# Transposing u of chunks 3 to 7 by VectorE's blocks and sixteen DMAs, with the next x product ahead of the new chunk's gates

## What is computed

```
t   = rmsnorm(x, norm1_w)
xb  = causal_depthwise_conv(t @ Wx, conv_w, conv_b)          # 4 taps
h   = rg_lru(xb, Wi, Wa, lam)                                # gates by sigmoid, a scan along the tokens
h1  = x + (h * gelu(t @ Wy)) @ Wo
u   = rmsnorm(h1, norm2_w)
ffn = (gelu(u @ Wg) * (u @ Wu)) @ Wd                         # Wg, Wu: 256 x 1024
x1  = layernorm(x + h1 + ffn)
out = layernorm(x1 + relu(x1 @ W1 + b1) @ W2 + b2)           # W1: 256 x 1024
```

## Time and profile before

| what | value |
|---|---|
| median of three runs | 587.22 us (586.84 to 587.23) |
| the profiled execution | 587.02 us |
| its span, first to last instruction | 585.2 us |
| TensorE busy | 578.5 us (99%) |
| VectorE, ScalarE, GpSimd busy | 401.0, 314.6, 203.8 us |
| granted TensorE clock, mean | 0.998 |

### The profile page before, as it was taken

How to read it: one execution, slowest core, us unless ns; L and a number is a source line. 1 busy time by engine, 2 the same in 40 slices (tenths; PEclk the granted TensorE clock), 3 DMA queues, 4 the chain that set the end, 5 groups by cost and what they waited for, 6 DMA issues and landing times.

```text
span 585.2 us, 9307 instructions
## 1 busy us (share of the span) xinstructions
PE 578.5 (99%) x3441; PEld 511.9 (87%) x3441; DVE 401.0 (69%) x729; ACT 314.6 (54%) x600; POOL 203.8 (35%) x282
## 2 busy tenths in 40 slices
PE   8999999999999999999999999999999999999996
PEld 8768988898888988898888888889888898888996
DVE  5888958867739668495765848568595765563565
ACT  7977675834548444573446634575343843232454
POOL 2111336273233542255233452424523233140130
PEclk9999999999999999999999999999999999999999
DMA  7400210011100121001210031100200010101011
GB/s 275 149 36 25 84 36 2 2 29 44 37 0 1 27 84 36 1 1 38 73 37 0 1 82 38 26 2 8 65 22 16 1 34 5 34 3 37 1 38 36
DMA packets 27197, 21.46 MB, mean 37 GB/s; under 512 B 3448, under 2 KB 26384, under 8 KB 27152
## 3 DMA queue, kind: packets, MB, share of 16 engines
q1 hardware_dynamic: 27152, 20.87, 11.8%
HBM read 10.89 MB, written 4.19 MB: 26 GB/s over the span
## 4 chain that ended last, share of the span: by engine, by line
PE 97%; DVE 1%; POOL 0%; issue 0%; ACT 0%; DVEq 0%; POOLq 0%; ACTq 0%
PE psum L454 18%; PE psum L456 18%; PE psum L455 18%; PE psum L465 11%; PE psum L467 11%; PE psum L466 11%; PE psum L545 2%; PE psum L472 1%; PE psum L838 1%; PE psum L510 1%; PE psum L676 1%; PE psum L678 1%; PE psum L674 1%; PE psum L572 1%; PE psum L529 1%; PE psum L489 0%
## 5 line engine op out<-in xcount | busy, mean ns | idle before, releaser
L1903 POOL TENSOR_SCALAR gu_hi<-gu_raw 128x512 fp32r<-128x512 f32 x64 | 54.4, 851 | 262.0 <-DVE gu_raw L1514 262.0
L1092 ACT ACTIVATE hid_raw<-psum,vecs 128x512 f32<-128x512 f32 x56 | 38.4, 686 | 115.4 <-PE psum L456 115.3
L1514 DVE TENSOR_TENSOR gu_raw<-psum,gu_raw 128x512 f32<-128x512 f32 x64 | 44.0, 687 | 69.9 <-PE psum L456 69.9
L1524 DVE TENSOR_TENSOR hid_lo<-hid_raw,hid_hi 128x512 fp32r<-128x512 f32 x56 | 40.7, 728 | 47.2 <-ACT hid_hi L1096 47.2
L465 PE MATMUL psum<-w_d_hi,gu_hi 128*128 128x256 f32 x256 | 72.2, 282 | 0.0
L465 PE MATMUL psum<-w_hi,hid_hi 128*128 128x256 f32 x256 | 71.9, 281 | 0.2 <-DVE hid_lo L1524 0.2
L467 PE MATMUL psum<-w_d_hi,gu_lo 128*128 128x256 f32 x256 | 71.8, 281 | 0.0
L467 PE MATMUL psum<-w_hi,hid_lo 128*128 128x256 f32 x256 | 71.8, 281 | 0.0
L466 PE MATMUL psum<-w_lo,hid_hi 128*128 128x256 f32 x256 | 71.7, 280 | 0.0
L466 PE MATMUL psum<-w_d_lo,gu_hi 128*128 128x256 f32 x256 | 71.7, 280 | 0.0
L1077 ACT ACTIVATE gu_raw<-psum 128x512 f32<-128x512 f32 x64 | 38.1, 595 | 50.3 <-PE psum L456 49.7
(11 more groups left out here) (237 smaller groups left out, 1530.7 us busy)
## 6 DMA issues: line engine op xcount, KB each, us to landing
out_dram<-row SPq DMA_DIRECT2D x15, 256.0 KB, 2.4
xs<-in_L_attn_x_dram SPq DMA_DIRECT2D x7, 512.0 KB, 3.7
gy<-normed SPq DMA_DIRECT2D x96, 32.0 KB, 1.9
t_raw<-t_blocks SPq DMA_DIRECT2D x80, 32.0 KB, 1.9
raw_gud<-in_L_attn_Wg_dram SPq DMA_DIRECT2D x1, 1024.0 KB, 8.1
raw_gud<-in_L_attn_Wu_dram SPq DMA_DIRECT2D x1, 1024.0 KB, 10.2
raw_gud<-in_L_attn_Wd_dram SPq DMA_DIRECT2D x1, 1024.0 KB, 12.4
raw_gud<-in_L_ffn_W_dram SPq DMA_DIRECT2D x1, 1024.0 KB, 6.6
```

What stands on the lines that cost most here:

```text
L1092: nc.scalar.activation(raw, hidden, ACT.Relu, bias=vec("b1", m)).then_inc(relu_ready, 1)
L1514: nc.vector.tensor_tensor(gu_raw[:, r % SLOTS, :], up_bank(r)[:, :], gu_raw[:, r % SLOTS, :], ALU.mult).then_inc(gu_ready, 1)
L1524: nc.vector.tensor_tensor(hid_lo[:, w % SLOTS, :], hid_raw[:, w % SLOTS, :], hid_hi[:, w % SLOTS, :].bitcast(FP32), ALU.subtract).then_inc ...
L1903: nc.gpsimd.tensor_scalar(gu_hi[:, r % SLOTS, :], gu_raw[:, r % SLOTS, :], 1.0, 0.0, ALU.mult, ALU.add).then_inc(gu_hi_ready, 1)
```

## The change

For chunks 3 to 7, `transpose_u` and the splits from PSUM are gone. VectorE makes u's 32x32 blocks into a new buffer, sixteen DMAs on SyncE's queue put them in place in another, and ScalarE and VectorE split u from there. The new buffers lie over `mT_hi` and `mT_lo`. The tokens of u come out in the order of the blocks; gelu of the gate and gate times up put them back in order (`in_order`, `by_token`). Around it steps are moved:

- `mix_x(n + 1)` stands at the end of round 7 of the period before, ahead of the new chunk's first gate; for that t of chunk n + 1 is made in round 4 (`norm_t`, blocks, DMAs) and split in round 6.
- `mix_y(n)` stands in round 4 between `up` and `down`.
- `norm_u` stands ahead of `gate_hi` on GpSimd in round 6.
- the statistics of the second layer norm go from round 4 to round 6, its normalising from round 6 to round 7.
- the first gate of a chunk waits for one low half of u before its first k step, and for the other before its second.

```diff
+        with nc.sbuf_tensor("u_blocks", [P, KD, T], FP32) as u_blocks, nc.sbuf_tensor("u_raw", [P, KD, T], FP32) as u_raw:
+            pass
         mT_hi = sb("mT_hi", [P, KD, T], FP32R)
...
+        def move_blocks(queue, src, dst, moved):
...
+            for i in range(GROUPS):
+                for j in range(GROUPS):
...
+                    queue.dma_start(placed[rows_out, :, i, :], blocks[rows_in, :, j, :]).then_inc(moved, DMA)
...
+            def move_u(c):
+                sync.wait_ge(u_blocks_ready, KD * (c - BLOCKWISE + 1))
+                move_blocks(sync, flat(u_blocks), flat(u_raw), u_blocks_moved)
...
                 if c >= 4:
+                    move_u(c - 1)
                     store_out(c - 4)
             for c in range(CHUNKS - 4, LAST - 1):
                 move_x1(c + 1)
+                if c + 3 < CHUNKS:
+                    move_u(c + 3)
                 store_out(c)
...
                 if m == 0:
-                    pe.wait_ge(uT_lo_ready, 2 * c + 2)
+                    pe.wait_ge(uT_lo_ready, 2 * c + (1 if c >= BLOCKWISE else 2))
...
-                product(gate_bank(r)[:, :], "g", m, uT_hi, uT_lo).then_inc(gate_done, 1)
+                for k in range(KD):
+                    if m == 0 and k == KD - 1:
+                        pe.wait_ge(uT_lo_ready, 2 * c + 2)
+                    last = product_step(gate_bank(r)[:, :], "g", m, k, uT_hi, uT_lo)
+                last.then_inc(gate_done, 1)
...
                     up(r)
+                if mixing and m == 4 and p >= 2:
+                    mix_y(n)
                 if mixing and m == 3 and p >= 1:
                     mix_decay(n)
-                if mixing and m == 7 and p >= 2:
-                    transpose_u(n)
...
-                if mixing and m == 0 and p >= 2:
+                if r == 2 * KH:
                     mix_x(n)
-                if mixing and m == 4 and p >= 1:
+                if m == 7 and p >= 2 and n + 1 < CHUNKS:
+                    mix_x(n + 1)
+                if r == KH + 4:
                     mix_y(n)
...
+            def split_u_hi(c):
+
+                act.wait_ge(up_done, KH * c)
+                act.wait_ge(u_blocks_moved, MOVES * (c - BLOCKWISE + 1))
+                for f in range(KD):
+                    nc.scalar.activation(uT_hi[:, f, :], u_raw[:, f, :], ACT.Copy).then_inc(uT_hi_ready, 1)
...
+                    if m == 6 and p >= 2 and n + 1 < CHUNKS:
+                        split_t_hi(n + 1)
...
+                    if m == 7 and p >= 2:
+                        split_u_hi(n)
...
+            def transpose_u_blocks(c):
+                dve.wait_ge(u_ready, u_tiles(c))
...
+                if m == 6 and second:
+                    statistics(s, 1, 0, s2_ready)
+                    statistics(s, 1, 1, s2_ready)
                 if units(r):
                     gate_times_up(r)
+                if m == 6 and p >= 2 and n + 1 < CHUNKS:
+                    split_t_lo(n + 1)
+                if m == 6 and mixing and p >= 2:
+                    transpose_u_blocks(n)
...
                     hidden_lo(w)
+                    if m == 4 and p >= 2 and n + 1 < CHUNKS:
+                        transpose_blocks(n + 1)
+                    if m == 7 and mixing and p >= 2:
+                        split_u_lo(n)
...
-                if p == 1 and m == 7:
+                if mixing and m == (7 if p == 1 else 6):
                     norm_u(n)
                 if r < UNITS:
                     gate_hi(r)
...
+                if m == 4 and p >= 2 and n + 1 < CHUNKS:
+                    norm_t(n + 1)
```

More of the change, by code:

```diff
@@ L381, in store_out @@
                                    rows[c % 2][:, 2 * q:2 * q + 2, :]).then_inc(out_stored[c % 2], DMA)
[L383 to L393, removed]
             def move_t(c):
                 sync.wait_ge(t_blocks_ready, KD * (c - BLOCKWISE + 1))
-                move_blocks(flat(t_blocks), flat(t_raw), t_blocks_moved)
+                move_blocks(sync, flat(t_blocks), flat(t_raw), t_blocks_moved)
             def move_x1(c):
                 sync.wait_ge(x1_blocks_ready, KD * c)
-                move_blocks(flat(normed), flat(gy), x1_blocks_moved)
+                move_blocks(sync, flat(normed), flat(gy), x1_blocks_moved)
+            def move_u(c):
+                sync.wait_ge(u_blocks_ready, KD * (c - BLOCKWISE + 1))
+                move_blocks(sync, flat(u_blocks), flat(u_raw), u_blocks_moved)
             for q in range(PAIRS):
@@ L1076, in gelu_gate @@
                     act.wait_ge(gu_lo_ready, r - SLOTS + 1)
-                nc.scalar.activation(gu_raw[:, r % SLOTS, :], gate_bank(r)[:, :],
+                dst, gate = gu_raw[:, r % SLOTS, :], gate_bank(r)[:, :]
+                if r >= KH * BLOCKWISE:
+                    dst, gate = by_token(dst), in_order(gate)
+                nc.scalar.activation(dst, gate,
                                      ACT.Gelu_apprx_tanh).then_inc(gelu_ready, 1)
@@ L1175, in round_of @@
                 mixing = n < CHUNKS
-                if mixing and m == 1:
+                if r == 2 * KH + 1 or r == KH + 1:
                     conv_start(n, 1)
@@ L1184, in round_of @@
                 if mixing:
-                    if m == 0 and p >= 2:
+                    if m == 6 and p >= 2 and n + 1 < CHUNKS:
+                        split_t_hi(n + 1)
+                    if r == 2 * KH:
                         split_t_hi(n)
@@ L1307, in transpose_blocks, with split_u_lo @@
                                         ).then_inc(t_blocks_ready, 1)
+            def transpose_u_blocks(c):
+                dve.wait_ge(u_ready, u_tiles(c))
+                for k in range(KD):
+                    nc.vector.transpose(u_blocks[:, k, :].rearrange("p (j t s) -> p t j s", j=GROUPS, t=TT),
+                                        normed[:, :, k * P:(k + 1) * P].rearrange("p t (j s) -> p t j s", j=GROUPS)
+                                        ).then_inc(u_blocks_ready, 1)
+            def split_u_lo(c):
+                for f in range(KD):
+                    dve.wait_ge(uT_hi_ready, 2 * c + f + 1)
+                    nc.vector.tensor_tensor(uT_lo[:, f, :], u_raw[:, f, :], uT_hi[:, f, :].bitcast(FP32),
+                                            ALU.subtract).then_inc(uT_lo_ready, 1)
             def transpose_x1_blocks(c):
-                dve.wait_ge(uT_done, 2 * (c + 2))
+                if c + 1 < BLOCKWISE:
+                    dve.wait_ge(uT_done, 2 * (c + 2))
+                else:
+                    dve.wait_ge(u_blocks_ready, KD * (c + 2 - BLOCKWISE))
                 dve.wait_ge(x1_ready, TT * c + TT)
@@ L1672, in round_of @@
                     split_x1_lo(f)
-                if m == 6 and second:
+                if m == 7 and second:
                     normalise(s, 1, 0, out_ready)
@@ L1691, in round_of @@
                         statistics(f, 0, 1, s1_ready)
-                if m == 4 and second:
-                    statistics(s, 1, 0, s2_ready)
-                    statistics(s, 1, 1, s2_ready)
                 if r == FROM:
@@ L1863, in norm_u @@
                 rms(h1_squares(c), ss2, h1_squared, rms2_ms, rstd2, rms2_rstd)
-                pool.wait_ge(uT_done, 2 * c)
+                if c <= BLOCKWISE:
+                    pool.wait_ge(uT_done, 2 * c)
+                else:
+                    pool.wait_ge(u_blocks_ready, KD * (c - BLOCKWISE))
                 if by_blocks(c - 2):
```

29 lines of the change are left out of this document (15 added, 14 removed).

## The result

The changed kernel takes 630.72 us (median of four runs, 627.63 to 631.67) against 587.23 for the kernel before beside it: 1.073 times as long, 95% interval 1.069 to 1.077. The forecast was 626.3. The profiled execution took 631.58 us, its span 629.8, against 587.02 and 585.2: 44.6 us more. The mean granted clock fell from 0.998 to 0.971.

The account below looks back on a forecast made before the run. TensorE's own work was taken to bound the kernel (97% of the chain). Profiled 587.0 - 4.4 (transposes) + 12.0 (Wo wait) + 23.7 (u wait) + 8 (clock) = 626.3 us, range 612 to 638.

Parts of the forecast that it names:

- its likeliest case: Whole kernel: both waits come and TensorE's clock mostly falls at the gates, 626.3 us with its bounds; chance 0.58.
- Transposes: TensorE: forty transposes of u removed from the chain, 0.87 us a chunk in five chunks, 4.4 us saved.
- Product with Wo: Round 5: early Wy delays relu, root, scan and low part; TensorE waits 2.4 us in five periods, 12.0 us.
- u: First gate of a period: TensorE waits for u's low part, 4.2 us four times and 6.9 once, 23.7 us.
- the quick norm: GpSimd's norm of u taking 3.31 instead of 4.47 us: gate waits of 3.0 and 5.7, together 17.7 us.
- The clock: TensorE after gate waits: clock falls, 2.0 us lost after the long wait, 1.5 after each of four others, 8 us.
- The long wait: Gate wait of the last period (chunk 7), without a next x product: 6.9 us, charged 2.0 us of clock.
- The sentence on the Trainium skill: TensorE's clock falling 5.2 us after the last matmul: only the 6.9 us wait would cost, 2.0 not 8, sum 620.3.
- the clock holds: Rival: both waits come, but TensorE's clock stays up or returns at once, 618.3 to 620.3 us; chance 0.22.
- only u: Rival: no wait ahead of Wo, because the relu's release does not set the root, 614.3 us; chance 0.07.
- only Wo: Rival: SyncE issues faster, u's leg is covered, 594.6 us, 2.7 more if chunk 7 lacks cover; chance 0.05.
- faster: Rival: TensorE's two waits a period sum to less than the 0.87 us saved, its deciding point; 582.6 us; chance 0.04.

Follow-up runs that it names:

- e7: The changed kernel with round 4 reordered, seven of u's DMAs on ScalarE's queue, t's low part later, nine extra matmuls before the last gate: 589.45 us, 1.0039 times before.
- e8: As e7, but chunk 7's u transposed by TensorE, no extra matmuls, and round 5's gate times up behind Wo's low part: 584.60 us against 587.13, 0.9956 times before.
- e1: The kernel before with only the Wy product of chunks 3 to 7 moved between up and down of round 4: 603.13 us, 1.0275 times before.
- e4: The changed kernel with round 4 reordered: root ahead of relu on ScalarE, t's blocks and scan ahead of hidden split on VectorE: 620.02 us, 1.056 times before.
- e5: The changed kernel with the x product back at its old place behind the gate: 642.40 us, 1.0935 times before.
- e2: The changed kernel with six of u's sixteen DMAs issued from ScalarE's queue instead of SyncE's: 605.06 us, 1.029 times before.
- e3: The changed kernel plus 30 unread identity matmuls (45 in the last period) on TensorE ahead of each period's first gate: 632.80 us, 1.076 to 1.081 times before.
- e6: As e3, with 15 unread identity matmuls (22 in the last period) in place of 30 (45): 622.67 us, 1.060 times before.

## Why the prediction was right, and which term was too small

The forecast, 626.3 in 612 to 638, held the measured 630.72, and its likeliest case is the one that came. Step by step:

- **Transposes, -4.4.** The rows of eight end with chunk 2 in the trace after. That they were worth their 0.87 us is borne out by the sums of e7 and e8, which close with them to 0.0 and 0.6 us.
- **Product with Wo, 12.0.** Measured 12.4 (2.45 to 2.5 a period). Relu, root and low part are each where the prediction put them, e1 shows that Wy's place alone does it, and e4 that the link is the order behind the relu, on ScalarE and VectorE together. That t's blocks add nothing was right as well: they fill the hole in which VectorE waits for the root (e1).
- **u, 23.7.** Measured 22.7. The leg in p = 3 is 1.84 + 4.39 + 1.34 + 12.9 = 20.5 us against 20.77 forecast, TensorE's cover 16.6 as forecast. That the norm's leg came out so near (4.39 against 4.47) is partly luck: its small steps took 1.50 us where the row used had 2.18, its four tiles 2.80 where it had 2.29. The last period was put at 6.9 and is 5.7: there is no t to split there, VectorE leaves GpSimd alone, and the norm's tiles take 1.86 us, near the quick norm, which I had used as a bound only (5.7).
- **The clock, 8.** This is the term that was mis-sized: 12.4 behind the gates and 1.5 behind one wait ahead of Wo, 13.9 us. That it would fall, and that the waits of 2.4 us are at the edge, was right. The step that failed is the price: "2.0 us lost" at the start of the kernel, from rows with a granted clock of 1.00, and 1.5 of it a gate. Nothing in the trace before could show how long the clock stays down once work is back. It is 5.1 to 5.9 us at four of the gates, 2.5 to 2.9 us lost each. The long wait, which I charged most, lost least (1.5). With the measured clock and the other terms as forecast the sum is 632.2, with all terms as measured 631.6; the profiled run took 631.58.

The sentence on the Trainium skill (TensorE: Matmul & The Clock Gate, part 1) would have had only the longest wait pay. The fall came 2.8 to 3.1 us after the last matmul in four waits and 5.1 us after in the last one, where the page's run has 5.2. The same part says that what is watched does not start anew when a kernel starts, and gives this as the reason why the moment of a change of the clock varies. That the moment of the fall varies agrees with these rows; the reason no run here shows.

The rivals: "the clock holds" fell by the windows, "only u" and "only Wo" by the two lines of waits, "faster" by both. Its point of decision was right, though: e7, with some 0.9 us left in each of four periods and 2.9 in the last, is a little slower than the kernel before, and e8, which brings both waits well under 0.87, is faster.

## What to carry to other kernels

Taking work off the engine that bounds a kernel pays only if what replaces it arrives in time: add up the leg of the replacement (here sixteen issues of 0.64 us on one queue) against what that engine has left to do before it needs the result. When a step is moved ahead on a busy in-order engine, look at every engine that takes something from behind it; here a product that changed its place by 2.7 us held a relu, and the relu held a root that had nothing to do with it. And a wait on TensorE is not over when it ends: price the time at half clock behind it as a term of its own, here 12.4 us behind 22.7 us of waits at the gates.

## What the runs showed of the hardware that I had not expected

- **The clock stays down.** After a wait of 3.9 to 4.8 us matmuls of 512 columns start 0.43 us apart in place of 0.23, for 5.1 to 5.9 us of uninterrupted work in the change, and for 3 us after a wait of 5.7. Across e4 and e5 the loss a gate went from 1.6 to 2.9 us, without order by the wait's length, and in these three kernels the fall came between 2.0 and 5.1 us after the last matmul.
- **A wait of 2.5 us (1.7 to 1.9 of it without any matmul) may or may not bring it down.** In the six kernels that have this wait ahead of Wo in five periods each (the change, e1, e2, e3, e5, e6) it fell behind 10 of the 30, at about 1.5 us each: none in e3's profile, three in e5's and e6's. Each time it fell only after TensorE had begun again, 0.1 to 1.6 us after. The change's runs lie 4 us apart (627.63 to 631.67), those of the kernel before 0.8, and the mean granted clock goes with the time: 0.979 in the run of 627.63, 0.974 in that of 629.86, 0.971 in the two slower ones, and in the same order in the runs of e1, e2, e3 and e5. So the time at half clock differs from run to run; at which waits, only the one trace of each kernel could show. What decides a single fall stays open.
- **Small DMAs between places in SBUF cost their issuer 0.64 us each,** on ScalarE's queue as on SyncE's, and two queues issue side by side (3.85 us for six beside 6.37 for ten).
- **The four tiles of GpSimd's norm took 2.80 us with VectorE's split of t beside them and 1.86 without** (p = 2 to 5 and p = 6 of the change). No run changes this alone.
